# Gathering the numerators of a group into one block over two banks, and turning the attend output on VectorE instead of TensorE

## The chip, the cores and the metric

One core of a Trainium2 chip runs the whole kernel. The metric is the device time of one execution in microseconds (us). The kernel before takes 3307.4 us as the median of three runs (3306.03 to 3308.24).

## What is computed

The input is `x` of 8 x 1024 x 512 in float32, 8192 rows in all. It is normalised to `xn`, and then two branches are added to it:

```python
def performer(xn):                       # 16 heads of 32, 128 random features
    pq, pk = phi(q * scale), phi(k * scale)     # phi(u) = exp(u @ omega.T - |u|^2/2 - max)/sqrt(128) + 1e-6
    kv = einsum('bhsm,bhsk->bhmk', pk, v);  z = sum(pk, axis=2)
    num = einsum('bhsm,bhmk->bhsk', pq, kv);  den = einsum('bhsm,bhm->bhs', pq, z)
    h = (num / den[..., None]) @ wo
    y = layernorm(xn + h, ln1_g, ln1_b)
    return layernorm(y + gelu(y @ w1 + b1) @ w2 + b2, ln2_g, ln2_b)

def gated(xn):                           # a step with the row before it
    r = sigmoid(mix_r(xn) @ W_r);  k = square(relu(mix_k(xn) @ W_k))
    return r * (k @ W_v)

out = x + performer(xn) + gated(xn)
```

## The kernel before

The rows are worked on in 32 groups of 256 (`TG` = 2 tiles of 128 rows), in three passes. The keys pass (up to about 840 us of the span) normalises the rows, makes queries, keys and values and sums `kv` and `z`. The attend pass (to about 1895 us) makes the numerators, the product with `wo`, the first layer norm and the gated branch, and stores `y` and `r`. The feed-forward pass (to the end) loads `y`, multiplies by `w1` and `w2` and writes the output. A float32 product of full size is made of three fp32r products, hi by hi, hi by lo and lo by hi (`product`, L185 to L190), so most operands exist as a pair of a rounded `hi` and a rest `lo`.

The order of work on every engine is written out by hand. `PE_BODY`, `DVE_BODY`, `ACT_BODY`, `POOL_BODY` and `SP_BODY` are lists of jobs (name, number, lead), and each engine runs through its list once for each group; a lead of -1 is the group before. Between two passes the `..._CROSSING` lists do the same. Semaphores tie the lists together, and each engine waits in its own order: an instruction that waits holds everything behind it.

**A group of the attend pass on TensorE (PE).** Two `max` blocks (feature products whose maximum is wanted, L1320), two `k`, two `r` and two `out` blocks of the gated branch (`gated` banks), the turn of `below` (L1328, into the PSUM bank `turn`), two `feat` blocks (the features themselves, L1338 in float32, and L1344, which adds `belowT` in fp32r; each for 256 columns at a time), four `num` blocks (numerators and denominators of four heads each, L1356), and two `wo` blocks with the group before. The four `num` blocks stand apart: `num` 0 behind the second `feat`, `num` 1 behind the second `out`, `num` 2 behind `wo`, `num` 3 behind the first `max` of the next group. All use the one bank `num`, and ScalarE empties it each time into `raw` (L1186).

**The chain to `wo`.** The denominators in `raw` go to DRAM and back, VectorE inverts them (`recip`, L1278), they go out and back again spread over the partitions, VectorE multiplies (`o`, L1281), ScalarE rounds (`oT` hi, L1191), and GpSimd subtracts (`oT_lo`, L1145). Only then `wo` may start. GpSimd runs in the order `diff`, two `k` rests (L1141), `norm` (gain and offset of `y`, four instructions, L1161 and L1163), the rest of the first mix (L1137), `oT_lo`, then the small `stats` and the rest of the second mix. Its job `part_sums` (L1152) comes in one group of four.

**VectorE in a group.** `top` twice, `recip`, `below`, `mix` 0, `exp` 0 (`pT`, L1274), `o`, `out` 0 and `out` 1 (L1285, they empty the `gated` banks and let `wo` in), `mix` 1, `hi` 1 (the second `pT`), `wo` 0 and 1 (`y` out of the banks, L1292), `stats`.

**A group of the feed-forward pass.** Eight `w1` blocks (24 matmuls each) and eight `w2` blocks (21 each) alternate. Between `w2` 4 and `w1` 7 PE turns the next group's `y` with eight transposes into two banks (`turn`, L1803). ScalarE and VectorE split the turned tiles (`yT_hi` L1626, `yT_lo` L1696), and `w1` 0 of the next group needs them. SyncE issues, behind the store of the output: the load of `y` (L1555), of `x` (L1560) and `r` (L1561), then the `tq` loads. `y` is loaded once VectorE has made `yb` from the one before (L1738). VectorE waits for `r` in `base` (L1729), and behind `base` stands its work for `w1` 6: four combinations, `ht_lo` (L1715), and the second `ht_lo` (L1724), which the fourth product of `w2` 6 needs (semaphore `s_lo`).

## Time and profile before

| | |
|---|---|
| median of the runs | 3307.4 us |
| the profiled execution | 3309.45 us, of which the span from first to last instruction is 3307.6 us |
| granted TensorE clock, mean | 0.994 |
| PE busy | 3246.5 us, 98% of the span |
| VectorE (DVE), ScalarE (ACT), GpSimd (POOL) busy | 69%, 50%, 33% |
| DMA | 409.60 MB, mean 124 GB/s |

Busy PE time is not the same as PE at its peak: matmuls overlap, and the busy time covers the filling and the emptying of the array between unlike blocks too. What a block costs is read from the distance between the start of its first matmul and that of the next block's.

### The profile page before, as it was taken

To read this page: it belongs to the slowest core of one execution; us is meant where nothing else is said; L and a number is where in the kernel's file an instruction comes from. 1 tells how busy PE (TensorE), PEld (TensorE's weight loads), DVE (VectorE), ACT (ScalarE), POOL (GpSimd) and SP (SyncE) were. 2 spreads that over 40 slices of the span, in tenths; PEclk is the share of its full clock that TensorE was granted. 3 is DMA by queue.
4 is the path that set the end of the run, shared out by engine and by line. 5 is a ranking of instruction groups with operands and counts; after the bars stand their busy time and mean duration, and the time that the engine had idled before them with its cause. 6 is when DMAs were issued, how large, how long until landed. Compare 5 with 4: busy or idle time off the path is not lost.

```text
span 3307.6 us, 73559 instructions
## 1 busy us (share of the span) xinstructions
PE 3246.5 (98%) x28521; PEld 2826.8 (85%) x28521; DVE 2279.7 (69%) x4678; ACT 1657.2 (50%) x3552; POOL 1086.0 (33%) x857
## 2 busy tenths in 40 slices
PE   7999999998899999999999999999999999999998
PEld 6777777777677777777777789999999999999998
DVE  6777777777567667676676666666666676676666
ACT  5666666666454545454545454443444443444443
POOL 3555554555355656565656430000000000000000
PEclk9999999999999999999999999999999999999999
DMA  3222222223344443434434463444444444444443
GB/s 122 95 87 76 102 87 86 95 87 95 105 103 120 109 122 100 129 92 126 111 108 117 137 223 133 146 150 150 147 153 147 151 143 153 139 139 142 150 147 128
DMA packets 250121, 409.60 MB, mean 124 GB/s; under 512 B 94512, under 2 KB 119600, under 8 KB 249776
## 3 DMA queue, kind: packets, MB, share of 16 engines
q1 hardware_dynamic: 249776, 404.90, 38.1%
q8 instruction: 229, 3.75, 0.5%
q14 instruction: 116, 0.95, 0.1%
HBM read 292.50 MB, written 112.33 MB: 122 GB/s over the span
## 4 chain that ended last, share of the span: by engine, by line
PE 72%; DVE 1%; issue 0%; POOL 0%; DMA 0%; ACT 0%; SPq 0%; DVEq 0%; POOLq 0%; ACTq 0%
PE ffn_hidden L188 32%; PE attend_gated L188 22%; PE ffn_result L188 8%; PE attend_num L1356 4%; PE attend_feat L1320 2%; PE attend_feat L1338 2%; PE ffn_turn L1803 1%; PE attend_feat L1344 1%; PE attend_turn L1328 0%; DVE ffn_yb L1770 0%; DMA den_d<-attend_raw 0%; DVE attend_top L1255 0%; DVE attend_below_parts L1268 0%; DVE attend_below_parts L1266 0%; POOL shared_y L1163 0%
## 5 line engine op out<-in xcount | busy, mean ns | idle before, releaser
L188 PE MATMUL ffn_hidden<-ffn_yT_hi,ffn_wa_hi 128*128 128x256 f32 x2048 | 574.1, 280 | 4.9 <-DVE ffn_wa_lo L1691 2.9
L188 PE MATMUL ffn_hidden<-ffn_yT_lo,ffn_wa_hi 128*128 128x256 f32 x2048 | 573.3, 280 | 0.0
L188 PE MATMUL ffn_hidden<-ffn_yT_hi,ffn_wa_lo 128*128 128x256 f32 x2048 | 572.1, 279 | 0.0
L329 POOL TENSOR_TENSOR ffn_n_rstd<-ffn_n_base,ffn_n_power 128x2 f32<-128x2 f32 x32 | 27.5, 860 | 1299.4 <-DVE ffn_n_negmean L324 1299.4
L188 PEld LDWEIGHTS ffn_hidden<-ffn_yT_hi,ffn_wa_hi 128*128 128x128 f32 x2048 | 385.0, 188 | 5.9 <-DVE ffn_wa_lo L1691 3.6
L188 PEld LDWEIGHTS ffn_hidden<-ffn_yT_hi,ffn_wa_lo 128*128 128x128 f32 x2048 | 385.2, 188 | 0.0
L188 PEld LDWEIGHTS ffn_hidden<-ffn_yT_lo,ffn_wa_hi 128*128 128x128 f32 x2048 | 384.9, 188 | 0.2
L1673 ACT ACTIVATE ffn_ht_hi<-ffn_hs 128x512 fp32r<-128x512 f32 x248 | 156.7, 632 | 409.9 <-DVE ffn_hs L1720 409.9
L1724 DVE TENSOR_TENSOR ffn_ht_lo<-ffn_hs,ffn_ht_hi 128x512 fp32r<-128x512 f32 x248 | 173.6, 700 | 219.2 <-ACT ffn_ht_hi L1673 219.2
L698 ACT ACTIVATE keys_e<-keys_feat,keys_below 128x128 f32<-128x128 f32 x1024 | 283.3, 412 | 54.6 <-DVE keys_below L763 54.6
L633 POOL TENSOR_TENSOR keys_z_sum<-keys_z_sum,keys_e 128x512 f32<-128x512 f32 x192 | 243.7, 1287 | 189.9 <-ACT keys_e L698 189.7
L1658 ACT ACTIVATE ffn_hid<-ffn_hidden,ffn_bias 128x256 f32<-128x256 f32 x496 | 206.4, 468 | 188.7 <-PE ffn_hidden L188 188.7
L759 DVE TENSOR_REDUCE keys_top<-keys_feat 128x4 f32<-128x512 f32 x256 | 158.8, 685 | 123.5 <-PE keys_feat L864 123.5
L1274 DVE TENSOR_SCALAR attend_pT_hi<-attend_feat 128x512 f32<-128x512 f32 x256 | 159.0, 683 | 77.2 <-ACT attend_feat L1171 75.5
L1186 ACT ACTIVATE attend_raw<-attend_num 128x512 f32<-128x512 f32 x128 | 76.6, 599 | 266.4 <-PE attend_num L1356 266.4
L188 PE MATMUL ffn_result<-ffn_wb_lo,ffn_ht_hi 128*128 128x256 f32 x744 | 209.2, 281 | 0.0
L188 PE MATMUL ffn_result<-ffn_wb_hi,ffn_ht_lo 128*128 128x256 f32 x744 | 208.8, 281 | 0.0
L188 PE MATMUL ffn_result<-ffn_wb_hi,ffn_ht_hi 128*128 128x256 f32 x744 | 208.0, 280 | 0.0
L1255 DVE TENSOR_REDUCE attend_top<-attend_feat 128x4 f32<-128x512 f32 x256 | 158.9, 685 | 69.2 <-PE attend_feat L1320 69.1
L188 PE MATMUL ffn_hidden<-ffn_tq,ffn_ht_hi 128*128 128x256 f32 x992 | 197.8, 281 | 0.0
L1667 ACT ACTIVATE ffn_ht_hi<-ffn_hid 128x384 fp32r<-128x384 f32 x248 | 130.7, 527 | 109.4 <-PE ffn_result L188 102.1
L188 PEld LDWEIGHTS ffn_hidden<-ffn_tq,ffn_ht_hi 128*128 128x128 f32 x992 | 151.7, 188 | 0.0
(274 smaller groups left out, 9560.7 us busy)
## 6 DMA issues: line engine op xcount, KB each, us to landing
ffn_tq<-part_d SPq DMA_DIRECT2D x248, 512.0 KB, 4.0
keys_xin<-in_L_attn_x_dram SPq DMA_DIRECT2D x32, 512.0 KB, 4.2
xn_d<-keys_xn SPq DMA_DIRECT2D x32, 512.0 KB, 2.8
xT_d<-keys_xT_whole SPq DMA_DIRECT2D x32, 512.0 KB, 2.6
u_d<-keys_uq_turned SPq DMA_DIRECT2D x32, 512.0 KB, 2.9
shared_xTf<-xT_d SPq DMA_DIRECT2D x32, 512.0 KB, 5.3
r_d<-shared_gate SPq DMA_DIRECT2D x32, 512.0 KB, 3.1
attend_o<-rden_d SPq DMA_DIRECT2D x128, 128.0 KB, 2.7
```

What stands on the lines that cost most here:

```text
L188: last = pe.matmul(out, stationary[a], moving[b], start=start and n == 0, stop=stop and n == len(TERMS) - 1)
L633: pool.tensor_tensor((z_all if last_of_batch else z_sum)[:, c, :], z_sum[:, c, :], e[t][:, c, :], ALU.add).then_inc(z_added[t], 1)
L698: last = act.activation(e[t][:, c, j * M:(j + 1) * M], feat[j].t[:, c * M:(c + 1) * M], ACT.Exp, bias=below[:, t, h:h + 1])
L759: dve.tensor_reduce(top[:, n, :, j:j + 1], feat[j].t[:, :].rearrange("p (c m) -> p c m", c=NC), AX.X, ALU.max).then_inc(top_ready, 1)
L1186: act.activation(raw[:, n, :], num.t[:, :], ACT.Copy).then_inc(num.free, 1)
L1255: dve.tensor_reduce(top[:, n, :, j:j + 1], feat[j].t[:, :].rearrange("p (c m) -> p c m", c=NC), AX.X, ALU.max).then_inc(feat[j].free, 1)
L1274: dve.tensor_scalar(pT[j][:, :], feat[j].t[:, :], FLOOR, None, ALU.add).then_inc(feat[j].free, 1)
L1356: last = pe.matmul(num.t[rows(j), part * GT:(part + 1) * GT], kvz[:, n, j, part * KD:(part + 1) * KD], pT[j][:, n % 2 * GT:(n % 2 + 1) * G ...
L1658: last = act.activation(hid[n % 2][:, 1 - a, :], bank.t[:, a * GT:(a + 1) * GT], ACT.Gelu, bias=bias1[:, 2 * n + a:2 * n + a + 1])
L1667: act.activation(ht[n % 2].hi[:, 0:3, :].rearrange("p q n -> p (q n)"), hid[n % 2][:, :, :].rearrange("p a n -> p (a n)")[:, 0:3 * P], ACT ...
L1673: act.activation(ht[n % 2].hi[:, 3:7, :], hs[:, :, :], ACT.Copy).then_inc(s_hi, 1)
L1724: dve.tensor_tensor(ht[n % 2].lo[:, 3:7, :], hs[:, :, :], f32(ht[n % 2].hi[:, 3:7, :]), ALU.subtract)\
```

## The change

The four `num` blocks of a group are moved to one place, behind `wo`, at the head of the next round of the list. They take turns in two PSUM banks, `num` and `turn`. So the second `pT` has a buffer of its own (`pT_late`).

In `feat` both halves of the float32 products now come first and the fp32r ones after them.

`y` is turned on VectorE: two transposes of 128x512 in 32x32 blocks, job `turn_y`, behind `out` 0. The result is stored to a new DRAM tensor `yT_d`. The feed-forward pass loads it already turned with four DMAs of 256 B runs (`load_turned`, as for the queries) into the tile `y_in`. PE's eight transposes are gone, and `yT_hi` and `yT_lo` are made from SBUF. The plain `y` is loaded later into the same tile, once `yT` is split. `out` 1 on VectorE moves behind `turn_y` and `hi` 1. In the attend pass `xn` and `y` are read and written with two neighbouring rows on a partition, so `wo` takes its stationary columns with a step of two.

```diff
+def by_pairs(dram):
+    return dram.rearrange("(g p t) d -> g p t d", t=TG, p=P)
...
-        PE_BODY = [("max", 0, 0), ("num", 3, -1), ("k", 0, 0), ("max", 1, 0), ("k", 1, 0), ("r", 0, 0),
-                   ("below", 0, 0), ("feat", 0, 0), ("r", 1, 0), ("out", 0, 0), ("feat", 1, 0),
-                   ("num", 0, 0), ("out", 1, 0), ("num", 1, 0), ("wo", 0, -1), ("wo", 1, -1),
-                   ("num", 2, 0)]
+        PE_BODY = [("num", 0, -1), ("num", 1, -1), ("num", 2, -1), ("num", 3, -1), ("max", 0, 0), ("k", 0, 0),
+                   ("max", 1, 0), ("k", 1, 0), ("r", 0, 0), ("below", 0, 0), ("feat", 0, 0), ("r", 1, 0), ("out", 0, 0),
+                   ("feat", 1, 0), ("out", 1, 0), ("wo", 0, -1), ("wo", 1, -1)]
...
+                if job == "store_yT":
+                    wait_alone(sp, y_turns, TG * g + TG, sp_passed)
+                    sp.dma_start(yT_d[g], y_turned[:, :, :, :].rearrange("p b j t -> p b (j t)")).then_inc(yT_stored, 16)
...
+                if job == "turn_y":
+                    wait(dve, yT_stored, 16 * g)
+                    for t in range(TG):
+                        dve.wait_ge(offsets, TG * g + t + 1)
+                        dve.transpose(y_turned[:, :, :, t], y[:, t, :].rearrange("p (b k) -> p b k", k=KD)).then_inc(y_turns, 1)
...
                 if job == "num":
                     if n == 0:
-                        pe.wait_ge(kvz_ready, 2 * b + 2)
-                    wait(pe, num.free, NC * g + n)
+                        pe.wait_ge(kvz_ready, 2 * (g // GB) + 2)
+                    if n == 1:
+                        pe.wait_ge(belowT_ready, g + 1)
+                    wait(pe, num.free, NC * g + n - 1)
...
-                            last = pe.matmul(num.t[rows(j), part * GT:(part + 1) * GT],
+                            last = pe.matmul(num_bank[n % 2][rows(j), part * GT:(part + 1) * GT],
                                              kvz[:, n, j, part * KD:(part + 1) * KD],
-                                             pT[j][:, n % 2 * GT:(n % 2 + 1) * GT], start=True, stop=True)
+                                             pT[n // 2][j][:, n % 2 * GT:(n % 2 + 1) * GT], start=True, stop=True)
...
-                        last = product(pe, gated[n].t[:, :], oT[:, c, n * P:(n + 1) * P], w["o"][:, c, :],
+                        last = product(pe, gated[n].t[:, :], [tile_of(part, n) for part in oT[:, c, :]], w["o"][:, c, :],
...
+                elif job == "yT":
+                    wait_alone(sp, yb_ready, g, sp_passed)
+                    load_turned(sp, y_flat, yT_d[g], yT_loaded)
+                if job == "y":
+                    wait_alone(sp, yT_ready, 2 * g + 2, sp_passed)
+                    sp.dma_start(y[:, :, :], y_g[g]).then_inc(y_loaded, 16)
...
-                if job == "turn":
-                    pe.wait_ge(y_loaded, 16 * g + 16)
```

On PE, in the attend pass, between the last matmuls of `wo` and the first `k` of the next group there stood this (`attend_num<-` are numerators, `shared_omegaT` as the first input is `max`):

```order
L188 MATMUL attend_gated<-shared_wo_lo,attend_oT_hi 128x512
L188 MATMUL attend_gated<-shared_wo_hi,attend_oT_lo 128x512
L1356 MATMUL attend_num<-attend_pT_hi,attend_kvz_hi 32x256 x8
L1320 MATMUL attend_feat<-shared_omegaT,shared_qT 128x128 x16
L1356 MATMUL attend_num<-attend_pT_hi,attend_kvz_hi 32x256 x8
L188 MATMUL attend_gated<-shared_mix_hi,shared_wk_hi 128x256
```

And now, at the same place:

```order
L189 MATMUL attend_gated<-shared_wo_lo,attend_oT_hi 128x512
L189 MATMUL attend_gated<-shared_wo_hi,attend_oT_lo 128x512
L1373 MATMUL attend_num<-attend_pT_hi,attend_kvz_hi 32x256 x8
L1373 MATMUL attend_turn<-attend_pT_hi,attend_kvz_hi 32x256 x8
L1373 MATMUL attend_num<-attend_pT_late,attend_kvz_hi 32x256 x8
L1373 MATMUL attend_turn<-attend_pT_late,attend_kvz_hi 32x256 x8
L1335 MATMUL attend_feat<-shared_omegaT,shared_qT 128x128 x16
L189 MATMUL attend_gated<-shared_mix_hi,shared_wk_hi 128x256
```

All four numerator blocks stand together, so neither the second `feat` and `out` nor `out` and `wo` have one between them any more, and `wo` comes up sooner behind `out`.

On VectorE, in the same pass, from the first `pT` of a group to the `y` of the group before, the order was:

```order
L1274 TENSOR_SCALAR attend_pT_hi<-attend_feat 128x512 x4
L1281 TENSOR_TENSOR attend_o<-attend_raw,attend_o 128x1024
L1285 SCALAR_TENSOR_TENSOR shared_gate<-shared_gate,attend_gated 128x512 x2
L1242 SCALAR_TENSOR_TENSOR shared_mixed<-shared_diff,shared_mu,shared_xTf 128x256 x4
L1251 COPY shared_xTf<-shared_xTf 128x4
L1274 TENSOR_SCALAR attend_pT_hi<-attend_feat 128x512 x4
L1292 TENSOR_TENSOR shared_y<-attend_gated,shared_xb 128x512 x2
```

And it is now:

```order
L1283 TENSOR_SCALAR attend_pT_hi<-attend_feat 128x512 x4
L1290 TENSOR_TENSOR attend_o<-attend_raw,attend_o 128x1024
L1294 SCALAR_TENSOR_TENSOR shared_gate<-shared_gate,attend_gated 128x512
L1308 STREAM_TRANSPOSE attend_y_turned<-shared_y 128x512 x2
L1283 TENSOR_SCALAR attend_pT_late<-attend_feat 128x512 x4
L1294 SCALAR_TENSOR_TENSOR shared_gate<-shared_gate,attend_gated 128x512
L1251 SCALAR_TENSOR_TENSOR shared_mixed<-shared_diff,shared_mu,shared_xTf 128x256 x4
L1260 COPY shared_xTf<-shared_xTf 128x4
L1302 TENSOR_TENSOR shared_y<-attend_gated,shared_xb 128x512 x2
```

Two transposes and the second `pT` now stand ahead of the second `out`.

On SyncE's queue, in the feed-forward pass, a group's loads behind the store of the output were:

```order
L1568 DMA out_dram<-ffn_x_in 128x2x512
L1555 DMA ffn_y_in<-y_d 128x2x512
L1560 DMA ffn_x_in<-in_L_attn_x_dram 128x2x512
L1561 DMA ffn_r_in<-r_d 128x2x512
L1545 DMA ffn_tq_14804<-part_d 128x1024
```

And they are now:

```order
L1592 DMA out_dram<-ffn_x_in 128x2x512
L142 DMA ffn_y_in<-yT_d 32x16x64 x4
L1584 DMA ffn_x_in<-in_L_attn_x_dram 128x2x512
L1585 DMA ffn_r_in<-r_d 128x2x512
L1571 DMA ffn_tq_14806<-part_d 128x1024
L1571 DMA ffn_tq_14804<-part_d 128x1024
L1571 DMA ffn_tq_14805<-part_d 128x1024
L1540 DMA ffn_y_in<-y_d 128x2x512
```

Four DMAs with runs of 64 elements stand where one with rows of 512 was, ahead of `x` and `r`, and the plain `y` follows three `tq` loads later.

## Rows read from the trace of the kernel before

**Rows 1.** The page: busy time by engine.

```profile
PE 3246.5 (98%) x28521; PEld 2826.8 (85%) x28521; DVE 2279.7 (69%) x4678; ACT 1657.2 (50%) x3552; POOL 1086.0 (33%) x857
```

**Rows 2.** Windows, three attend groups: us; busy PE, PEld, DVE, ACT, POOL.

```profile
1467.54:1500.28 32.74, 32.74 (x303) 25.19 (x299) 21.82 (x43) 16.17 (x26) 19.03 (x12) 1.00 0.37 118
1500.28:1532.82 32.54, 32.54 (x303) 24.98 (x299) 20.61 (x41) 16.68 (x28) 18.44 (x12) 1.00 0.47 125
1532.82:1565.78 32.96, 32.96 (x303) 25.29 (x299) 26.55 (x41) 16.06 (x26) 20.96 (x16) 1.00 0.47 110
```

**Rows 3.** Timeline of PE, one attend group: start, length, instruction.

```profile
1513.22 0.39 PE L1344 MATMUL attend_feat<-attend_belowT,attend_pick 32*128 32x256 f32 x4
...
1522.15 0.50 PE L188 MATMUL attend_gated<-shared_wv_hi,attend_ka_hi 128*128 128x512 f32 x1
1522.49 0.40 PE L188 MATMUL attend_gated<-shared_wv_lo,attend_ka_hi 128*128 128x512 f32 x1
1522.73 0.40 PE L188 MATMUL attend_gated<-shared_wv_hi,attend_ka_lo 128*128 128x512 f32 x1
...
1524.83 0.40 PE L188 MATMUL attend_gated<-shared_wv_hi,attend_ka_lo 128*128 128x512 f32 x1
1525.15 1.07 PE L1356 MATMUL attend_num<-attend_pT_hi,attend_kvz_hi 128*32 128x256 f32 x16
1526.15 0.50 PE L188 MATMUL attend_gated<-shared_wo_hi,attend_oT_hi 128*128 128x512 f32 x1
```

**Rows 4.** One `num` block (min/median/max ns, first and last start), then ScalarE's timeline.

```profile
L1356 PE MATMUL attend_num<-attend_pT_hi,attend_kvz_hi x16: 379/379/403, 1521.2 to 1521.8; 128*32 128x256 f32 x16
...
1512.79 0.39 ACT L1178 ACTIVATE attend_belowT<-attend_turn 128x256 fp32r<-128x256 f32 x1 [0.96 <-PE attend_turn L1328]
...
1522.29 0.60 ACT L1186 ACTIVATE attend_raw<-attend_num 128x512 f32<-128x512 f32 x1 [1.68 <-PE attend_num L1356]
```

**Rows 5.** Timeline of GpSimd, then of VectorE, in that group.

```profile
1518.40 3.35 POOL L1137 TENSOR_TENSOR shared_mix_lo<-shared_mixed,shared_mix_hi 128x1024 fp32r<-128x1024 f32 x1
1521.71 2.40 POOL L1145 TENSOR_TENSOR attend_oT_lo<-attend_o,attend_oT_hi 128x1024 fp32r<-128x1024 f32 x1
...
1517.22 2.30 DVE L1281 TENSOR_TENSOR attend_o<-attend_raw,attend_o 128x1024 f32<-128x1024 f32 x1
```

**Rows 6.** VectorE's transposes in the keys pass: min/median/max ns.

```profile
L750 DVE STREAM_TRANSPOSE keys_uq_turned<-keys_uq x64: 666/686/706, 32.0 to 801.9; 128x512 f32<-128x512 f32 x64
```

**Rows 7.** PE, a feed-forward group: `w1` 5, 6, 7 begin; fourth product of `w2` 6.

```profile
2105.93 0.28 PE L188 MATMUL ffn_hidden<-ffn_yT_hi,ffn_wa_hi 128*128 128x256 f32 x1
...
2111.21 0.28 PE L188 MATMUL ffn_hidden<-ffn_yT_hi,ffn_wa_hi 128*128 128x256 f32 x1
...
2117.32 0.36 PE L188 MATMUL ffn_hidden<-ffn_yT_hi,ffn_wa_hi 128*128 128x256 f32 x1
...
2123.73 0.28 PE L188 MATMUL ffn_hidden<-ffn_wb_hi,ffn_ht_hi 128*128 128x256 f32 x1
```

**Rows 8.** SyncE's queue in that group, and its turned loads in the attend pass.

```profile
2107.34 0.39 SPq L1568 DMA_DIRECT2D out_dram<-ffn_x_in  x1
2108.81 0.37 SPq L1555 DMA_DIRECT2D ffn_y_in<-y_d  x1
...
L141 SPq DMA_DIRECT2D shared_qT<-u_d x64: 567/636/2397, 819.9 to 1792.1; - x64
```

**Rows 9.** DMA: GB/s in 40 slices of 1460 to 1472 us, then of 2105 to 2122 us.

```profile
GB/s 0 0 0 0 0 27 137 382 375 403 375 75 0 31 205 355 372 331 366 305 250 213 213 171 174 205 183 89 29 6 0 0 0 0 82 0 0 0 0 51
...
GB/s 0 0 0 0 39 0 0 120 390 386 328 43 202 366 323 308 193 251 260 207 207 193 342 405 434 419 390 352 405 405 318 337 299 357 164 116 96 19 0 39
```

**Rows 10.** VectorE's waits for `r` (us, times, longest), then its timeline in that group.

```profile
DVE ffn_x_in L1729 <- DMA ffn_r_in<-r_d: 80.9, 32, 4.1
...
2117.50 1.23 DVE L1729 SCALAR_TENSOR_TENSOR ffn_x_in<-ffn_r_in,ffn_x_in 128x1024 f32<-128x1024 f32 x1 [3.29 <-DMA ffn_r_in<-r_d]
...
2121.97 0.69 DVE L1724 TENSOR_TENSOR ffn_ht_lo<-ffn_hs,ffn_ht_hi 128x512 fp32r<-128x512 f32 x1 [0.70 <-ACT ffn_ht_hi L1673]
```

More of the change, by code:

```diff
@@ L1439, in feed_forward_pass @@
         result.append(Bank(mem, ctx, "result1"))
-        turn = [Bank(mem, ctx, f"turn{n}") for n in range(2)]
         sums = [result[0].t, hidden[2].t, hidden[3].t, result[1].t]
@@ L1808, in do @@
                     if n == 0:
-                        for m in range(2):
-                            pe.wait_ge(turn[m].free, g + 1)
+                        pe.wait_ge(yT_ready, 2 * g + 2)
                     if g == 0:
```

152 lines of the change are left out of this document (75 added, 77 removed), and 5 rows, old and new, of tables (FFN_OVER, KEYS_OVER, PE_CROSSING).

## Prediction

> **What bounds the kernel now.** I began with the page. PE is busy for 98% of the span, the next engine for 69% [rows 1], so time is won only where PE's own work gets shorter, and lost where PE begins to wait. The windows of three attend groups say the same at close range: PE is busy for the whole of 32.74, 32.54 and 32.96 us [rows 2]. The third is a group in which GpSimd has its `part_sums` (20.96 us busy in place of 18.44) and VectorE is busier too: the chain to `wo` is longer there. Busy time hides the filling and emptying between unlike blocks, so each block is priced from PE's timeline by distance between starts [rows 3], and the neighbours' timelines say when they would be ready for an earlier PE [rows 4, 5]. The feed-forward pass is read the same way [rows 7], with SyncE's queue, the rate of the transfers and VectorE's waits [rows 8 to 10].
>
> **Attend pass, what PE saves.** The reader is to compare starts.
> - One numerator block takes 1526.15 − 1525.15 = 1.00 us alone [rows 3]. Its 16 matmuls are four waves; they start from 1521.2 to 1521.8 [rows 4], so about 0.22 apart, 0.88 for four. The other 0.12 is the join, and three of four joins go: 0.36. Against this, the third and fourth block need the bank of the first and second. ScalarE began to empty the shown block at 1522.29 and took 0.60 [rows 4]: free 1.74 after the block's start at about 1521.15, where the third wants it at 2 x 0.88 = 1.76. With a hand-over I count 0.06 of waiting in a group: −0.30.
> - The last `out` matmul stands 0.32 ahead of the numerators, where like matmuls stand 0.24 apart, and the first behind a block stands 0.34 from its neighbour [rows 3]. `wo` directly behind `out` saves both, 0.10 and 0.11: −0.21.
> - In `feat`, the first fp32r wave starts at 1513.22 [rows 3], and ScalarE finishes `belowT` at 1512.79 + 0.39 = 1513.18 [rows 4]: the wave waited for it. With both float32 halves ahead, two more waves lie over that wait. I put −0.14 on it; the bound below is 0, above the same with a second switch saved, 0.25.
>
> PE alone is then 0.65 shorter. If nothing else were late, a group would take 31.9.
>
> **Who is late next.** With two blocks (2.00) gone from ahead of `wo`, and the joins and `feat` (0.24), `wo` would start at 1526.15 − 2.24 = 1523.91. GpSimd ends `oT_lo` at 1521.71 + 2.40 = 1524.11 [rows 5]. That slack was 2.04 before, and becomes −0.20. GpSimd's own chain starts from `k` and does not move up, so PE waits 0.25 with the semaphore, and the group gains 0.40. In the eight groups with `part_sums`, 0.42 of the period, 32.96 against 32.54 [rows 2], comes from VectorE and GpSimd holding up the second `feat`; with the second `pT` in a buffer of its own and ahead of `out` 1 most of it goes: 0.70. Sum: 24 x 0.40 + 8 x 0.70 = −15.2; with the 0.2 that a fourth of the groups lose elsewhere (32.74 against 32.54 [rows 2]) −16. Ends: −22 if PE never waits for `oT_lo`, 0 below.
>
> **What VectorE gets.** Two transposes of 128x512: 666 to 706 ns each, in 64 cases of the keys pass [rows 6], so 1.38 a group. Behind them wait the second `pT` and `out` 1, which lets `wo` 1 in. VectorE is busy for 21.82, 20.61 and 26.55 us of the three groups (the third engine of a window, behind PE and its weight loads [rows 2]), so some 6 to 12 us are idle. `o` ends at 1519.52 [rows 5]; with `out` 0, two transposes, four `pT` and `out` 1 behind it, `out` 1 ends at about 1525, ahead of `wo` 1, which comes 2.9 after `wo` 0. Nothing. The store to `yT_d` stands behind `store_r` on SyncE and nobody in the pass waits for it. By-pairs loads and stores have longer runs: nothing. The stationary columns with a step of two: no row has them. The 24 products of `wo` hide their weight loads now; I take 0, and if each start came 0.02 later it would be 0.5 a group, which is the third rival below.
>
> **Feed-forward pass, what PE saves.** From `w1` 5 to `w1` 6 it is 2111.21 − 2105.93 = 5.28, from `w1` 6 to `w1` 7 2117.32 − 2111.21 = 6.11 with the turn inside: 0.83. The first matmul behind the turn is 0.08 longer, 0.36 against 0.28 [rows 7]. So 0.90 a group, 31 groups: −27.9.
>
> **What it pays for that.** The load of `y` was one issue of 0.37 behind the store of the output; the turned form takes 0.636 each in the attend pass [rows 8], so four take 2.54, from 2108.81 to 2111.35. `x` and `r` stand behind it. The transfer is slower too. Turned loads in the attend pass run at 171 to 250 GB/s, plain ones at 331 to 403 (first line of [rows 9]); and the plain `y` came at 202 to 366 (second line of [rows 9]). 0.52 MB at 200 takes 2.6 us instead of 1.4 to 1.7: later by 0.9 to 1.2; by pure halving of the rate 1.4. `x` and `r` land later by this, and I take 1.2. Ends: 0, if `r` overtakes the `tq` transfers that now run beside it, and 2.2, the whole issue time (2.54 − 0.37) if nothing overlaps.
>
> VectorE already waits for `r`: 80.9 us in 32 times, 2.53 each, 3.29 in the shown group [rows 10]. So a late `r` moves `base` one for one. Behind `base` stands the work for `w1` 6, whose last piece, the second `ht_lo`, runs from 2121.97 to 2122.66 [rows 10]. PE needs it for the fourth product of `w2` 6, at 2123.73 [rows 7], and without the turn at 2122.83. That leaves 0.17 in the shown group, and 0.17 + 3.29 − 2.53 = 0.93 in the mean one. With `r` later by 1.2 PE stalls 1.03 in the one and 0.27 in the other; since the groups spread (longest wait 4.1 [rows 10]) I estimate 0.5. Net 0.4 a group: 31 x 0.4 = −12.4. It is steep: at 0.5 later the pass gains 25, at 2.0 it loses 9 (stall 1.2).
>
> The Trainium skill, page *DMA: Bandwidth & Descriptors*, section Specifications, gives 512 B as the least transfer for line rate and a read-modify-write below it, which speaks against the 256 B runs. Rows 9 agree, 171 to 250 GB/s beside 331 to 403; by the rule alone the rate would be halved, 1.4 later, and the pass would gain 8 instead of 12.
>
> The plain `y` is loaded behind the `tq` loads; `yb` wants it some 20 us later: hidden. The split from SBUF instead of PSUM costs VectorE and ScalarE the same within 0.1. Between the passes one turn goes: −1.
>
> **Sum.** −16 − 12.4 − 1 = −29.4 on the profiled 3309.45, that is 3280.0. This execution (span and 1.85 around it) stands 2.05 above the median, so on the median's scale 3307.4 − 29 = 3278.
>
> **The rivals.**
> - *The turned load is hidden.* `r` comes up to 0.5 later, because the store of the output holds back `x` anyway. Then the feed-forward pass gains about 25 and the kernel takes 3266. For it: the queue has free slices between the transfers [rows 9]. Against it: `x` is issued behind all four.
> - *`base` eats the turn.* `r` comes 2.0 to 2.3 later: the pass loses 9 to 20, attend and the crossing gain 17: 3299 to 3311. For it: the wait for `r` stands in 32 of 32 groups [rows 10].
> - *The gain of attend is lost at the bank, at `oT_lo` or in `wo` itself.* If ScalarE, which must empty four blocks in a row at 1.1 + 0.60 each, is late for each pair, or `oT_lo` comes 0.5 later, only −1 is left there: 3294.
> - *The transposes hold up GpSimd* (the other side). GpSimd's `mix_lo` takes 3.35, where `oT_lo` of the same shape takes 2.40, and VectorE's `o` lies over its first 1.12 us [rows 5]: something shared is held. If the transposes, which now lie from about 1520.4 to 1521.8 at the end of `mix_lo` and the start of `oT_lo`, do the same, `oT_lo` ends 1.38 later, and `wo` waits 1.6: the group loses 0.9 in place of gaining, +30 over 32 groups. With −13.4 elsewhere 3324. It decides from 0.92 later on, where attend's loss of 32 x (0.92 − 0.50) equals 13.4. Against it: the transposes of the keys pass take 666 to 706 with no tail [rows 6], and `o` reads two tensors of SBUF where a transpose reads one.
>
> The Trainium skill, page *SBUF — State Buffer*, section *SBUF: two separate sides*, has that pair of ports as an exclusive lock between GpSimd and a VectorE operation that has two SBUF inputs or runs in a 2-port mode. The 3.35 against 2.40 of rows 5 agrees; by the rule the one-input transpose takes no lock, and the last rival does not come.
>
> **How the numbers follow.** Both gains with part of the second paid back: 0.45, 3278, by itself 3268 to 3291. Load hidden: 0.20, 3266. `base` eats the turn: 0.15, around 3305. Attend's gain lost: 0.10, 3294. Transposes hold GpSimd: 0.06, 3324. The rest, 0.04, is divided. From 3257 (load hidden and `oT_lo` not late: 3307.4 − 22 − 27.9) to 3305 (half of the third case) it holds 8 in 10. A measurement of this kernel can tell about 0.2%, 6.6 us: faster means below 3300.8. That takes the first, second and nearly all of the fourth case and a third of the third: 0.79. Within: half of the third and little else, 0.11. Slower: the last and the rest of the third, 0.10.
>
> **What the profile would show.** Right: four numerator blocks within 3.6 to 3.7 us; `wo` at most 0.4 after `out`; GpSimd's `oT_lo` as the new releaser of `wo`; an attend group of 32.1; `mix_lo` 3.3 to 3.4 and `oT_lo` 2.4 long as before; `w1` 6 to `w1` 7 in 5.3 us; VectorE's wait for `r` longer by 1.2 a group, and PE waiting about 0.5 for the second `ht_lo`, a group of some 42.8 against 43.2. Wrong: `mix_lo` or `oT_lo` longer by about 1, a third numerator block that starts over 2 us after the first, or a feed-forward group at 42.3 or above 43.3. Most would hang on how late `r` lands.

## The result and the profile after

The changed kernel takes 3278.56 us as the median of four runs (3277.38 to 3283.3) against 3307.01 (3306.03 to 3308.24) for the kernel before in the same runs: 0.9917 of it, 95% interval 0.9902 to 0.9932. That is 28.5 us less, where 29 less was forecast. The profiled execution has a span of 3276.3 us, 31.3 less than that of before.

The page of the changed kernel, with the line that answers to [rows 1], and the head of its chain of waits by engine:

```profile
PE 3213.0 (98%) x28265; PEld 2818.2 (86%) x28265; DVE 2259.3 (69%) x4742; ACT 1656.6 (51%) x3552; POOL 1087.9 (33%) x857
...
PE 45%; POOL 9%; DVE 7%; issue 4%; DMA 4%; ACT 3%; SPq 2%; DVEq 0%; ACTq 0%; POOLq 0%
```

PE is busy for 33.5 us less and still for 98% of the span. But the chain that ended last now passes through GpSimd for 9% and through VectorE for 7%, where it was 0% and 1% before: somebody else has begun to set PE's pace. To see where, the execution is cut at four points that both kernels have: the first `max` block of the first and of the last group of the attend pass, and `base` of the second and of the last feed-forward group. Windows of the kernel before (us, then busy time of PE, its weight loads, VectorE, ScalarE, GpSimd, then granted clock, DMA share, GB/s):

```profile
842.95:1859.84 1016.89, 1010.97 (x9199) 775.64 (x9199) 687.17 (x1244) 508.98 (x833) 583.96 (x402) 1.00 0.41 111
1859.84:1985.04 125.20, 117.83 (x904) 102.53 (x901) 81.21 (x123) 63.65 (x104) 46.65 (x30) 1.00 0.65 209
1985.04:3281.69 1296.65, 1296.65 (x11046) 1296.65 (x11046) 886.13 (x2040) 535.81 (x1082) 34.96 (x60) 1.00 0.43 146
```

and of the changed kernel:

```profile
843.25:1845.37 1002.12, 996.95 (x9214) 788.90 (x9214) 666.32 (x1309) 510.14 (x834) 589.52 (x403) 1.00 0.46 128
1845.37:1971.45 126.08, 118.01 (x878) 104.54 (x875) 81.95 (x122) 62.89 (x103) 43.49 (x30) 0.97 0.73 228
1971.45:3249.15 1277.70, 1274.35 (x10799) 1270.79 (x10798) 885.84 (x2040) 535.64 (x1080) 34.90 (x60) 1.00 0.49 161
```

The attend pass gained 14.8 us (16 forecast), the crossing lost 0.9 (a gain of 1 forecast), and thirty feed-forward groups gained 18.95, 0.63 each (0.40 forecast, 12.4 for 31). The keys pass lost 0.3 and the end behind the last `base` 1.2. The sum of these is −31.3, the difference of the spans. One block stands on different sides of the second cut: `num` 3 came behind that `max` before and comes ahead of it now. With this 1.0 us on the same side, the attend pass gained 15.8 and the crossing lost 1.9.

**One attend group.** Windows that answer to [rows 2], an ordinary group and one with `part_sums`:

```profile
1489.03:1521.37 32.34, 32.28 (x302) 25.52 (x299) 22.02 (x42) 16.60 (x28) 18.43 (x13) 1.00 0.51 140
1521.37:1553.80 32.43, 32.28 (x302) 25.51 (x298) 21.48 (x42) 17.18 (x28) 21.37 (x17) 1.00 0.52 129
```

All groups are alike now, 32.3 to 32.4. Of three kinds before, 32.54, 32.74 and 32.96, the ordinary kind gained only 0.13 to 0.2. PE's timeline of the first of these groups, from the last `out` matmul on, answers to [rows 3]:

```profile
1511.46 0.40 PE L189 MATMUL attend_gated<-shared_wv_hi,attend_ka_lo 128*128 128x512 f32 x1
1511.92 0.51 PE L189 MATMUL attend_gated<-shared_wo_hi,attend_oT_hi 128*128 128x512 f32 x1
1512.27 0.39 PE L189 MATMUL attend_gated<-shared_wo_lo,attend_oT_hi 128*128 128x512 f32 x1
...
1517.72 1.07 PE L1373 MATMUL attend_num<-attend_pT_hi,attend_kvz_hi 128*32 128x256 f32 x16
1518.61 1.05 PE L1373 MATMUL attend_turn<-attend_pT_hi,attend_kvz_hi 128*32 128x256 f32 x16
1519.51 1.07 PE L1373 MATMUL attend_num<-attend_pT_late,attend_kvz_hi 128*32 128x256 f32 x16
1520.39 1.05 PE L1373 MATMUL attend_turn<-attend_pT_late,attend_kvz_hi 128*32 128x256 f32 x16
1521.37 0.51 PE L1335 MATMUL attend_feat<-shared_omegaT,attend_uq 32*128 32x128 f32 x6
```

The four numerator blocks take 1521.37 − 1517.72 = 3.65 us, as forecast (4.00 before), and the third block doesn't wait for its bank: 0.90 and 0.88 from start to start. GpSimd's timeline in that group, and VectorE's transposes, answer to [rows 5, 6]:

```profile
1506.14 3.37 POOL L1146 TENSOR_TENSOR shared_mix_lo<-shared_mixed,shared_mix_hi 128x1024 fp32r<-128x1024 f32 x1
1509.47 2.40 POOL L1154 TENSOR_TENSOR attend_oT_lo<-attend_o,attend_oT_hi 128x1024 fp32r<-128x1024 f32 x1
...
1508.20 1.30 DVE L1308 STREAM_TRANSPOSE attend_y_turned<-shared_y 128x512 f32<-128x512 f32 x2
```

`oT_lo` ends at 1511.87 and `wo` starts at 1511.92. The same 0.05 stands between the two in all groups in the middle of the pass; before the change it was 2.05 in most of them. The transposes lie over the last part of `mix_lo`, which is as long as in [rows 5] (3.37 against 3.35). This is one group in four, though. In the next three `mix_lo` takes 2.4, and the last instruction of `norm` on GpSimd takes 2.2 to 2.4 instead of 1.3; in the second of them, GpSimd and VectorE:

```profile
1569.65 2.36 POOL L1172 TENSOR_TENSOR shared_y<-shared_y,attend_offset 128x512 f32<-128x512 f32 x1
1571.97 2.38 POOL L1146 TENSOR_TENSOR shared_mix_lo<-shared_mixed,shared_mix_hi 128x1024 fp32r<-128x1024 f32 x1
...
1569.62 1.22 DVE L1290 TENSOR_TENSOR attend_o<-attend_raw,attend_o 128x1024 f32<-128x1024 f32 x1
...
1572.99 1.30 DVE L1308 STREAM_TRANSPOSE attend_y_turned<-shared_y 128x512 f32<-128x512 f32 x2
```

`o` costs GpSimd's chain about 1 us either way; what changes from group to group is which of its instructions pays. Both transposes lie wholly over this `mix_lo`, which takes 2.38.

**One feed-forward group.** SyncE's queue, then VectorE, where the wait for `r` was longest; these answer to [rows 8, 10]:

```profile
2133.69 0.39 SPq L1592 DMA_DIRECT2D out_dram<-ffn_x_in  x1
2135.08 2.60 SPq L142 DMA_DIRECT2D ffn_y_in<-yT_d  x4
2137.80 0.56 SPq L1584 DMA_DIRECT2D ffn_x_in<-in_L_attn_x_dram  x1
...
2145.09 1.23 DVE L1753 SCALAR_TENSOR_TENSOR ffn_x_in<-ffn_r_in,ffn_x_in 128x1024 f32<-128x1024 f32 x1 [4.54 <-DMA ffn_r_in<-r_d]
```

`x` is issued 4.1 behind the store of the output, where it was 3.0 (2107.34 to 2110.35). VectorE's and PE's waits say what became of it:

```profile
DVE ffn_x_in L1753 <- DMA ffn_r_in<-r_d: 103.7, 32, 5.1
PE ffn_hidden L189 <- DVE ffn_ht_lo L1748: 2.4, 10, 0.3
```

VectorE waits 3.24 in place of 2.53 for `r`. PE stops at `ht_lo` in about half of the groups. The list above counts only the time in which PE has nothing in flight; the distances between its starts show 0.28 us a group in the mean. In the group shown `w1` 7 starts 5.32 behind `w1` 6, where it was 6.11 with the turn between them.

### The profile page after: what moved, and what is told of

Its sections match the earlier page's. It is cut to its first block, busy times and chain, and to the rows that moved or that the text cites. A ratio compares the mean times of both kernels' runs of the same rounds, so it can differ in the third digit from the quotient of the medians.

```text
span 3276.3 us, 73388 instructions
## 1 busy us (share of the span) xinstructions
PE 3213.0 (98%) x28265; PEld 2818.2 (86%) x28265; DVE 2259.3 (69%) x4742; ACT 1656.6 (51%) x3552; POOL 1087.9 (33%) x857
## 4 chain that ended last, share of the span: by engine, by line
PE 45%; POOL 9%; DVE 7%; issue 4%; DMA 4%; ACT 3%; SPq 2%; DVEq 0%; ACTq 0%; POOLq 0%
PE ffn_hidden L189 21%; PE attend_gated L189 13%; PE ffn_result L189 5%; POOL shared_y L1172 3%; PE attend_feat L1335 2%; POOL shared_y L1170 2%; POOL attend_oT_lo L1154 2%; DMA ffn_r_in<-r_d 2%; PE attend_num L1373 2%; PE attend_turn L1373 2%; DVE ffn_yb L1794 2%; POOL attend_ka_lo L1150 1%; ACT ffn_ht_hi L1697 1%; POOL shared_mix_lo L1146 1%; SPq L142 1%
## 5 line engine op out<-in xcount | busy, mean ns | idle before, releaser
L1180 ACT ACTIVATE attend_feat<-attend_feat 128x512 f32<-128x512 f32 x256 | 131.3, 588 | 59.2 <-PE attend_feat L1359 59.2
L189 PE MATMUL attend_gated<-shared_mix_hi,shared_wk_hi 128*128 128x256 f32 x512 | 151.8, 297 | 0.0
```

The lines of the kernel that those rows point to most:

```text
L189: last = pe.matmul(out, stationary[a], moving[b], start=start and n == 0, stop=stop and n == len(TERMS) - 1)
L1180: act.activation(feat[j].t[:, :], feat[j].t[:, :], ACT.Exp).then_inc(e_ready[j], 1)
```

## The experiments

**Each half alone.** `attend_only` has the changed attend pass without the turned `y`, and the old feed-forward pass:

```diff
-                    ("o", 0, -1), ("out", 0, 0), ("turn_y", 0, -2), ("hi", 1, 0), ("out", 1, 0), ...
+                    ("o", 0, -1), ("out", 0, 0), ("hi", 1, 0), ("out", 1, 0), ...
-                   ..., ("store_r", 0, 0), ("store_yT", 0, -2),
+                   ..., ("store_r", 0, 0),
+                   ("w1", 6, 0), ("w2", 4, 0), ("turn", 0, 1), ("w1", 7, 0), ("w2", 5, 0),
```

> The attend pass as in the changed kernel, but without the transposes and the store of the turned y; the feed-forward pass as before, with the eight transposes on TensorE. Theory: between the traces of before and after, the attend pass gave back 14.8 us up to its last group and the thirty feed-forward groups 19.0; if the two are independent, this kernel keeps the first alone: 3307 - 14 = 3293 (3290 to 3296), attend groups of 32.4 us, feed-forward groups of 43.2. Rival: the store and the transposes cost the attend pass something that the trace doesn't show as waiting (the transposes hold GpSimd, or the store crowds its loads); then the groups here are shorter than 32.4 and the kernel is below 3290.

Measured: 3292.06 (0.9954 of before, 0.994 to 0.9969), attend groups of 32.4, feed-forward groups of 43.3. The theory held. The transposes and their store cost the attend pass nothing: behind its first two groups, which differ in the granted clock (64.9 us together at 0.95 here, 62.6 at 0.96 in the changed kernel), it takes 939.3 us without them and 939.5 with them. The crossing is shorter here, 121.5 us against 126.1; part of that may be the clock, 0.99 in it here and 0.97 there.

`ffn_only` is the other half: the old order in attend, the new feed-forward pass, and the transposes on VectorE behind the second `pT` (the diff is against the old order).

```diff
-                    ("out", 1, 0), ("mix", 1, 1), ("hi", 1, 0), ("wo", 0, -1), ("wo", 1, -1),
+                    ("out", 1, 0), ("mix", 1, 1), ("hi", 1, 0), ("turn_y", 0, -2), ("wo", 0, -1), ("wo", 1, -1),
```

> The order of the attend pass as before (four numerator blocks apart, one bank, feat in the old order), with the two transposes and the store of the turned y added behind the second pT on VectorE, and the feed-forward pass as in the changed kernel. Theory: attend groups stay at 32.5 to 32.9 us, the feed-forward groups fall to 42.6: 3307 - 18 = 3289 (3286 to 3293). Rival: the old attend pass has the cover for the transposes only because its order was changed with them (VectorE is busy for 26.55 us in one group of four); then these groups grow by up to 1.4 us each in eight groups, and the kernel is at 3300.

Measured: 3346.67 (1.0122, 1.0099 to 1.0145), far above both expectations, although the feed-forward groups fell to 42.6. Groups of the attend pass took up to 39.2 us. SyncE's queue ahead of one of 37.9, whose first `max` block starts at 1013.46:

```profile
1006.54 0.37 SPq L1120 DMA_DIRECT2D r_d<-shared_gate  x1
1011.95 0.33 SPq L1126 DMA_DIRECT2D yT_d<-attend_y_turned  x1
...
1014.45 4.12 SPq L142 DMA_DIRECT2D shared_qT<-u_d  x4
1018.68 0.64 SPq L1095 DMA_DIRECT2D den_d<-attend_raw  x1
```

The timeline of VectorE and PE in that group, where they waited:

```profile
1010.56 1.30 DVE L1311 STREAM_TRANSPOSE attend_y_turned<-shared_y 128x512 f32<-128x512 f32 x2
...
1025.48 0.35 DVE L1290 RECIPROCAL attend_rden<-attend_den 128x32 f32<-128x32 f32 x1 [3.07 <-DMA attend_den<-den_d]
...
1029.13 0.44 PE L1346 MATMUL attend_turn<-shared_ident,attend_below_parts 128*128 128x128 f32 x2 [3.41 <-DVE attend_below_parts L1280]
```

The store of the turned `y` stands behind the store of `r` and waits 5 us more, until the transposes are done at 1011.86. The loads for the next group stand behind it, and behind those the first trip of the denominators, issued 5.2 us into the group where it is 3.0 in the kernel of the next experiment. `recip` on VectorE waits for them and holds up `below`, for which PE waits. A store that nobody waits for had come to the head of a queue.

These waits are only the larger part of the loss. The attend pass of this kernel, a piece of it behind the wait that ends at 1409.83, and the attend pass of the next kernel:

```profile
843.32:1918.75 1075.43, 1034.54 (x9199) 792.55 (x9199) 743.50 (x1302) 508.95 (x833) 583.01 (x402) 0.97 0.42 119
1409.00:1415.80 6.80, 5.97 (x33) 4.41 (x34) 6.59 (x9) 4.33 (x9) 3.23 (x3) 0.50 0.68 219
...
841.51:1860.24 1018.73, 1014.68 (x9198) 781.19 (x9198) 719.48 (x1302) 507.74 (x833) 584.41 (x402) 0.99 0.45 126
```

Of the 57 us between them PE spent 37 waiting for `below`, in 13 groups, and was busy for 20 more with the same matmuls. Ten of the 13 waits have a stretch of 3.4 to 6.8 us at the lower level of the clock, 1.2 GHz, that begins within 1.4 us of the wait's end.

`ffn_only_early` moves the two transposes back to where the changed kernel has them:

```diff
-                    ("o", 0, -1), ("out", 0, 0), ("out", 1, 0), ("mix", 1, 1), ("hi", 1, 0), ("turn_y", 0, -2),
+                    ("o", 0, -1), ("out", 0, 0), ("turn_y", 0, -2), ("out", 1, 0), ("mix", 1, 1), ("hi", 1, 0),
```

> As ffn_only (old order of the attend pass, turned y added, new feed-forward pass), with the two transposes behind out 0 on VectorE, where the changed kernel has them, instead of behind the second pT. In ffn_only the store of the turned y waited for the transposes in SyncE's queue, the loads of the next group stood behind it, and TensorE waited 38 us for VectorE's below. Theory: that head of the line is the whole loss of ffn_only; with the transposes some 9 us earlier the store no longer waits, attend groups are back at 32.5 to 33.0 us, and the kernel takes 3289 (3286 to 3294). Rival: the loss is VectorE's own time (1.4 us a group in an order with little room); then groups stay above 33.5 and the kernel above 3310.

Measured: 3295.04 (0.9961, 0.9947 to 0.9975), attend groups of 32.67, 32.83 and 33.07. The queue was the loss, with the clock that fell behind its waits. The time is 1 above the expected range; each group is still 0.13 longer than before, 4 us in all, and `columns` below finds that. The two halves give 14.9 and 13.4 us against the kernel before in their own runs, 28.3 together, and the whole change 28.5. That fits two independent halves, though each of these gains is known only to about 5 us.

**Who sets the pace in attend.** `pool_order` exchanges two jobs on GpSimd in the changed kernel:

```diff
-        POOL_BODY = [..., ("norm", 0, -2), ("mix", 0, 1), ("oT", 0, -1),
+        POOL_BODY = [..., ("norm", 0, -2), ("oT", 0, -1), ("mix", 0, 1),
```

> The changed kernel with one pair exchanged on GpSimd: oT_lo of the group before runs ahead of the rest of the first mix. Theory: in the changed kernel TensorE reaches wo about 0.3 us before oT_lo ends in every group, and pays 0.1 more for the restart; oT_hi is ready 1.1 us before GpSimd begins oT_lo. Ahead of mix_lo it ends about 1.1 earlier, the wait goes, attend groups fall from 32.4 to 32.0, and the kernel to 3278 - 12 = 3266 (3264 to 3270). Rival: TensorE's wait at wo has another last releaser (the second out evacuation on VectorE): then groups stay at 32.3 to 32.4 and the time within 2 us of 3278. A third: mix_lo, now later by 2.4, holds up the next k, and the groups get longer.

Measured: 3267.55 (0.9877, 0.9861 to 0.9894), every attend group from the third on 32.03, and GpSimd gone from the chain that ended last (0% for 9%). The wait was GpSimd's. GpSimd and VectorE in such a group, and then PE at `wo`:

```profile
1504.24 2.41 POOL L1154 TENSOR_TENSOR attend_oT_lo<-attend_o,attend_oT_hi 128x1024 fp32r<-128x1024 f32 x1 [2.25 <-ACT attend_oT_hi L1200]
1506.62 2.38 POOL L1146 TENSOR_TENSOR shared_mix_lo<-shared_mixed,shared_mix_hi 128x1024 fp32r<-128x1024 f32 x1
...
1500.79 2.29 DVE L1290 TENSOR_TENSOR attend_o<-attend_raw,attend_o 128x1024 f32<-128x1024 f32 x1
...
1504.04 1.30 DVE L1308 STREAM_TRANSPOSE attend_y_turned<-shared_y 128x512 f32<-128x512 f32 x2
...
1507.30 0.39 PE L189 MATMUL attend_gated<-shared_wv_hi,attend_ka_lo 128*128 128x512 f32 x1
1507.53 0.39 PE L189 MATMUL attend_gated<-shared_wo_hi,attend_oT_hi 128*128 128x512 f32 x1
1507.76 0.39 PE L189 MATMUL attend_gated<-shared_wo_lo,attend_oT_hi 128*128 128x512 f32 x1
```

`wo` follows `out` after 0.23, its second matmul after another 0.23 where it was 0.35 behind a wait: the wait costs its own length and 0.11 of restart. The group shows two more things. `mix_lo` no longer lies beside VectorE's `o` and takes 2.38, where it took 3.37 in this kind of group, one in four. (In the other three `o` still lies over `norm`; there the gain is that `oT_lo` comes ahead of the 2.4 of `mix_lo`.) And the transposes lie over the first half of `oT_lo`, which takes 2.41, as ever.

`feat_undone` puts the old order of `feat` back into the changed kernel, `feat_undone_pool` into `pool_order`:

```diff
                     for c in range(2):
                         for j in range(HC):
                             ...
-                    pe.wait_ge(belowT_ready, g + 1)
-                    for c in range(2):
+                        if c == 0 and n == 0:
+                            pe.wait_ge(belowT_ready, g + 1)
                         for j in range(HC):
                             last = pe.matmul(feat[j].t[:, cols], pick[rows(j), 2 * n + c, :], ...
```

> The changed kernel with the feat blocks in the order of before (float32, fp32r, float32, fp32r). Theory: TensorE does 0.10 us more in a group, but ahead of a wo that waits 0.3 for oT_lo anyway, so the group stays at 32.4 and the kernel within 1 us of 3278. Rival: TensorE sets the pace by itself; then 31 x 0.10 = 3 us slower, 3281.

> The same old feat order, but with oT_lo ahead of the rest of the first mix on GpSimd, where wo no longer waits. Theory: now the 0.10 us counts in full: groups of 32.13 against 32.03 in pool_order, and 3267.5 + 3 = 3270.7. Rival: no difference to pool_order here either, so the order of feat has no price at all.

Measured: 3279.49 and 3268.79, each about 1 us above its partner, which these runs can't tell from nothing. The groups tell more: 32.35, or 32.52 in those with `part_sums`, against 32.3 to 32.4 in the first, 32.09 against 32.03 in the second. The first `feat` block is 0.10 longer in both. Where `wo` waits, this 0.10 comes off the wait; where it doesn't, the group grows by 0.06, since the `r` block behind `feat` became 0.03 shorter. The direction is the theory's; the 3 us expected in the second are 2 by its groups.

`one_bank` lets all four numerator blocks use the bank `num`:

```diff
-        num_bank = [num.t, turn]
+        num_bank = [num.t, num.t]
-                    wait(pe, num.free, NC * g + n - 1)
+                    wait(pe, num.free, NC * g + n)
```

> The changed kernel with all four numerator blocks in the one bank num, one behind another. Theory: each block then waits for ScalarE to empty the bank, which began 1.1 us after the block's first matmul and took 0.6 in the trace of before; three of the four starts come about 0.85 to 0.95 us later, a group grows by 2.6 to 2.9 us, less the 0.4 that TensorE loses at wo now: 32.4 + 2.3 = 34.7, and the kernel takes 3278 + 70 = 3348. Rival: ScalarE follows closely enough that the restart alone counts, 0.3 a block: 3278 + 28 - 12 = 3294.

Measured: 3367.57 (1.0176, 1.0161 to 1.0191), where 3348 was expected. PE's numerator blocks in a group:

```profile
1538.05 1.07 PE L1373 MATMUL attend_num<-attend_pT_hi,attend_kvz_hi 128*32 128x256 f32 x16
1539.88 1.07 PE L1373 MATMUL attend_num<-attend_pT_hi,attend_kvz_hi 128*32 128x256 f32 x16 [0.76 <-issue]
1541.66 1.07 PE L1373 MATMUL attend_num<-attend_pT_late,attend_kvz_hi 128*32 128x256 f32 x16 [0.71 <-ACT attend_raw L1195]
```

From start to start it is 1.83 and 1.78 in place of 0.9; the four take 6.40, 2.75 more, as expected. But nothing of it is taken off the wait at `wo`: groups are 35.1, not 34.7. The block stands ahead of `k`, and GpSimd's chain starts from `k`, so the whole chain moves with it. That part of the expectation was wrong in its place, by 0.4 us a group.

`columns` is `attend_only` with `pool_order`'s exchange and with rows kept by groups instead of by pairs:

```diff
-    xn_g, y_g, r_g = by_pairs(xn_d), by_pairs(y_d), by_group(r_d)
+    xn_g, y_g, r_g = by_group(xn_d), by_group(y_d), by_group(r_d)
-                        last = product(pe, gated[n].t[:, :], [tile_of(part, n) for part in oT[:, c, :]], w["o"][:, c, :],
+                        last = product(pe, gated[n].t[:, :], oT[:, c, n * P:(n + 1) * P], w["o"][:, c, :],
```

> As attend_only (attend pass of the changed kernel without the turned y, feed-forward pass as before), with oT_lo ahead of mix_lo on GpSimd, and with xn and y read and written by groups again, so that wo takes neighbouring stationary columns instead of every second one. Theory: the step of two costs 0.13 us in the two wo blocks of a group: they take 5.79 us with it and 5.66 without it in the old order, and 5.69 with it directly behind out. Without it they take 5.56, the group 31.90 instead of 32.03, and the kernel 3292 - 12 - 4 = 3276. Rival: the 0.13 comes from something else in those kernels (the order of the blocks, the store of the turned y); then wo stays at 5.69 and the group at 32.03, 3280.

Measured: 3273.22 (0.9896, 0.9879 to 0.9912), where 3276 was expected, the two `wo` blocks together 5.54 us in place of 5.69 in `pool_order`. A window over one of its groups, and one over a group of `pool_order`:

```profile
1508.71:1540.58 31.87, 31.87 (x302) 25.46 (x299) 20.29 (x40) 17.19 (x28) 21.40 (x17) 1.00 0.44 111
```

```profile
1491.60:1523.63 32.03, 32.03 (x300) 25.59 (x299) 22.12 (x43) 16.61 (x28) 19.31 (x16) 1.00 0.49 142
```

The step of two in `wo`'s stationary columns costs 0.15 us a group, 0.006 for each of the 24 products. Nothing waits in either group; it is PE's own time. `columns` lacks the turned `y` too, but that has no part in it: `wo` takes 5.80 in the changed kernel and in `attend_only`. In the old order the same step costs 0.13 (5.79 in `ffn_only_early`, 5.66 before).

**What the turned load costs.** `yT_behind_r` issues it behind `x` and `r`:

```diff
-                    if 0 < g < G - 1:
-                        do("yT", 0, g + 1)
                     wait_alone(sp, base_ready, g, sp_passed)
                     ...
                     sp.dma_start(r_in[:, :, :], r_g[g]).then_inc(xr_loaded, 16)
+                    if 0 < g < G - 1:
+                        do("yT", 0, g + 1)
```

> The changed kernel with the four DMAs of the turned y issued behind x and r instead of ahead of them. Theory: r lands 0.7 us later than before behind them, and that costs TensorE 0.28 us in the mean of the feed-forward groups, at the two ht_lo of w1 6; behind r they cost nothing, since ScalarE reads the turned y only some 4 us after r has landed. VectorE's wait for r falls from 3.2 to 2.5 us or less, the groups from 42.61 to 42.33, the kernel to 3278 - 8 = 3270 (3268 to 3273). Rival: the load itself is late now and ScalarE waits for it, with the next w1 behind it: groups of 42.6 or more and a time of 3278 or above.

Measured: 3287.13 (0.9942, 0.9927 to 0.9957), slower than the changed kernel by 8.6. Both explanations fell: the time is the rival's, but ScalarE waited for the turned `y` only 0.2 us in all. VectorE's wait for `r` went as the theory had it, and lower, but PE had a new one:

```profile
DVE ffn_x_in L1753 <- DMA ffn_r_in<-r_d: 54.6, 32, 5.1
...
PE ffn_hidden L189 <- DMA ffn_tq<-part_d: 15.8, 19, 1.9
```

Three `tq` loads stand behind all this in the same queue, and PE needs them for `w2` soon after. In the changed kernel PE waits 0.5 for them in all.

`split` issues two of the four DMAs ahead of `x` and two behind `r`:

```diff
-                        do("yT", 0, g + 1)
+                        do("yT", 1, g + 1)
                     ...
                     sp.dma_start(r_in[:, :, :], r_g[g]).then_inc(xr_loaded, 16)
+                    if 0 < g < G - 1:
+                        do("yT", 2, g + 1)
 ...
-                    load_turned(sp, y_flat, yT_d[g], yT_loaded)
+                    load_turned(sp, y_flat, yT_d[g], yT_loaded, (range(HC), range(0, 2), range(2, HC))[n if g > 1 else 0])
```

> The changed kernel with two of the four DMAs of the turned y ahead of x and r and two behind them. Theory: x can't be issued before the store of the output has landed, 3.0 us after its issue; four issues of the turned y end 4.2 after it, two end at about 2.9. So x and r are issued 1.1 us earlier, the stall of 0.28 us a group at ht_lo nearly goes, and tq, which made TensorE wait 15.8 us when all four stood behind r, is issued no later than now: feed-forward groups of 42.4, the kernel at 3278 - 6 = 3272 (3269 to 3275). Rival: what makes r late is the slow transfer and not the issues; then r lands at most 0.4 earlier and the time stays within 3 us of 3278. Third: tq is late here too, and TensorE waits for it.

Measured: 3275.11 (0.9902, 0.9888 to 0.9917). It is 3.5 below the changed kernel, which these runs do not settle (the intervals overlap). `x` was issued 3.0 behind the store, VectorE's waits for `r` fell to 78.4 us, and PE's waits for `tq` rose to 5.0. `split_pool` joins it with `pool_order`:

> The two edits that helped, together: oT_lo ahead of the rest of the first mix on GpSimd, and the turned y loaded two DMAs ahead of x and r and two behind. Theory: they act in different passes and add up: 3278.5 - 11 - 3 = 3264 (3261 to 3267). Rival: one of them is within the spread of the measurement, and the kernel is at pool_order's 3267.5 or above.

Measured: 3267.66 (0.9875, 0.9861 to 0.989), the time of `pool_order` alone. The rival was right. PE waits 7.0 us for `tq` in nine groups. Thirty feed-forward groups took 1280.7 us here, 1276.6 in `split` and 1277.7 in the changed kernel. The six other traces with the changed feed-forward pass untouched have 1274.6 to 1280.4, so none of these three stands apart. What `split` takes from the wait for `r` it hands in part to `tq`; a net gain is not shown.

`long_runs` keeps four issues and the bytes, but reads runs of 4 KB; the rows then come in another order, so the output is another:

```diff
+        sp.dma_start(dst[b * KD:(b + 1) * KD, :, :].rearrange("p c n -> p (c n)"),
+                     src[b * KD:(b + 1) * KD, :, :].rearrange("p h k -> p (h k)")).then_inc(loaded, 16)
```

> The changed kernel with the four loads of the turned y reading 4 KB runs instead of 256 B ones: the same bytes and the same four issues, but the rows are not turned into the order the products need, so the output is another. Theory: what makes r late is the four issues ahead of x (x is issued 4.3 us behind the store of the output instead of 3.1), not the short runs; then r lands within 0.3 us of where it does now, base stays 10.0 to 10.2 us behind the issue of the store, and the time within 3 us of 3278. Rival: the short runs cost the time; then base comes 0.7 us or more earlier, the stall of 0.28 us a group goes, and the kernel takes 3270 or less.

Measured: 3270.18 (0.9884, 0.987 to 0.9899), the rival's time. The issues by line, 256 B runs in the changed kernel and 4 KB runs here (min/median/max ns):

```profile
L142 SPq DMA_DIRECT2D ffn_y_in<-yT_d x128: 562/630/1649, 1865.7 to 3202.7; - x128
```

```profile
L149 SPq DMA_DIRECT2D ffn_y_in<-yT_d x124: 317/416/1504, 1926.5 to 3197.5; - x124
```

My theory had set issues and runs against each other. They are one thing: an issue with short runs takes 630 ns, one with long runs 416, so `x` is issued 3.4 behind the store instead of 4.3, `base` comes 9.2 behind it instead of 10.2, and PE's stall is 0.02 us a group. Its thirty feed-forward groups take 1271.3 us, below all of the traces above. `r` is issued 1.0 earlier, and `base` comes 5.4 behind its issue in both kernels, so the whole gain stands in the issues.

## Why the prediction was right, and where only the sum was

**The attend pass: 16 forecast, 14.8 measured (15.8 with the same blocks on both sides of the cut), but not by the steps named.** The terms as written, 15.2 and eight times 0.2, make 16.8. PE's own work was put at 0.65 less. The numerators gave 0.35 (0.30 forecast) and `feat` 0.10 (0.14). The term "`wo` directly behind `out` saves both" gave 0.10 at the end of `out` and 0.12 in `wo` (0.21 forecast, though the rows shown, 0.32 and 0.34 against 0.24, make 0.18). But the step of two in `wo`'s columns cost 0.15, a cost for which I took 0 since no row had it. PE's work is 0.51 shorter, 32.03 (`pool_order`). "Who is late next" named the right operation, `oT_lo`, and sized its price wrongly: 0.25 forecast, 0.40 measured (32.43 against 32.03), of which 0.11 is the restart of `wo` after a wait. So `wo` stands 0.46 behind the last `out` matmul, beyond the 0.4 named as the sign, and the group takes 32.4, not 32.1. Together the ordinary group gained 0.13 to 0.2, where 0.40 was forecast.

The sum came close by luck. The groups with `part_sums` gained 0.53 each and the other slow kind 0.32, both less than their terms had it (0.70 and 0.60). But three groups, which no term of the sum covers, cost more in the kernel before than any of their kind:

```profile
842.95:876.49 33.54, 28.48 (x259) 21.69 (x259) 20.45 (x35) 14.49 (x25) 14.72 (x17) 0.91 0.44 103
876.49:910.76 34.27, 34.27 (x303) 25.93 (x299) 17.94 (x35) 14.65 (x24) 13.07 (x9) 0.94 0.40 97
1400.84:1435.00 34.16, 33.30 (x302) 25.20 (x298) 27.74 (x41) 16.10 (x26) 20.71 (x16) 1.00 0.40 104
```

In the changed kernel they take 30.61, 32.02 and 32.44, the first at a granted clock of 0.93, the others at 1.00. These three are 6.9 of the 14.8 us; the other 28 gave 7.9, or 0.28 each, where the terms of the sum, spread over them, make about 14. The first two are faster in the traces with the new order too, but by how much varies, and with it the clock: together 62.1 to 65.0 us in ten traces (`one_bank` aside), 67.4 to 67.8 in the three with the old order. The third, slow in the kernel before, is not so by the order: in `ffn_only_early`, which has the old order, it takes 33.05 like its kind. What made it slow is open.

**The feed-forward pass: 12.4 forecast, 19 measured.** The eight transposes and the restart were worth 0.90 a group as the rows said. The term that was mis-sized is the delay of `r`: 1.2 forecast, 0.67 measured (`base` stands 10.22 behind the store of the output in the mean, 9.55 before). The issue of `x` was later by 1.1, near the 1.0 that the rows give. The issue of `r` was later by 1.3. But `r` then landed sooner behind it, `base` 5.35 after its issue against 5.98. Why is not shown; the least is 5.10, in `yT_behind_r`, where no load of `y` stands ahead. The stall came to 0.28 instead of 0.5. The rule "mean group 0.93 of slack, shown group 0.17" held: PE stops in half the groups, and next to never without the delay (`long_runs`). The Trainium skill's 512 B, page *DMA: Bandwidth & Descriptors*, section Specifications, pointed the right way: in `long_runs` thirty groups take 1271.3 us against 1277.7, and the kernel 3270.2 against 3278.6. But what the long runs saved there was time of the issue, not of the transfer. The skill's mechanism, the read-modify-write, no run here shows, and the halving of the rate in the prediction was an estimate of mine: the page names no factor.

**Around the passes: −1 forecast, +2.4 measured** (crossing 0.9, end 1.2, keys 0.3). Without the turned `y` the crossing takes 121.5, 4.6 less. Some of this is work that SyncE and VectorE got, some may be the granted clock, 0.97 in the crossing of the changed kernel, 0.99 in that of `attend_only` and 1.00 before; the runs don't part them. The feed-forward pass gave 6.6 us more than forecast, the attend pass 1.2 and the rest 3.4 less: the errors cancel in part, and the total is met better than its terms.

**The rivals.** That the transposes hold up GpSimd fell: `mix_lo` takes 2.38 with both over it, `oT_lo` 2.41, and `attend_only`, which has no transposes, has the same 3.36 in one group of four and 2.38 in the others. What holds GpSimd is `o`, at `mix_lo` or at `norm`, and `o` itself takes 2.3 where GpSimd's instruction began first and 1.22 where `o` did. The Trainium skill, page *SBUF — State Buffer*, section *SBUF: two separate sides*, has the lock for an operation with two SBUF inputs, as `o` is, and not for one with a single input; both agree. That `base` eats the turn did not come, its delay was a third of what it needed. That the gain of attend is lost came in part: the ordinary group did lose most of it at `oT_lo` and in `wo`. The sentence "nobody in the pass waits for it", of the store to `yT_d`, is true for the place it has and false as a rule: in `ffn_only` waiting in the queue it cost some 50 us (3346.67 against 3295.04), some 20 of them in matmuls at a lower granted clock behind PE's waits.

**The best version** is `pool_order`, 3267.55: 39.4 less than before where the change alone gives 28.5, with two jobs of GpSimd exchanged.

## What to carry to other kernels

When blocks are taken out from ahead of a product, compute what the operand of that product needs on its own chain; if that chain starts from something that doesn't move up, the gain stops there, and the next thing to look at is the order on the engine that ends it. A wait costs more than its length (0.11 of restart at `wo`, and the clock in `ffn_only`), and a DMA that nobody waits for is a cost as soon as it waits itself in a shared queue. Of a layout chosen for one transfer (here rows by pairs, runs of 256 B), price what it does to the others: to the stationary columns of a product, to the time of an issue, and to the queue behind it.
